# One signal a tile for the left-over sums of a graph convolution

## The reference

```python
def gcn_conv(x, edge_index, W, b, n_nodes):
    ...
    norm = dinv[src] * dinv[dst]
    h = x @ W.T
    msg = h[src] * norm[:, None]
    out = jax.ops.segment_sum(msg, dst, num_segments=n_nodes)
    return out + b
...
    h = gcn_conv(x, edge_index, W1, b1, N_NODES)
    h = jax.nn.relu(h)
    out = gcn_conv(h, edge_index, W2, b2, N_NODES)
...
    x = x + _L0_gnn_ref(_layernorm(x, axis=-1), edge_index, ...)
    x = x + _L0_ffn_ref(_layernorm(x, axis=-1)[None], ...)[0]
```

## Time and profile before

| | |
|---|---|
| median of three executions | 2862.25 us (2860.14 to 2864.53) |
| the profiled execution, its own time | 2881.27 us |
| its span, first to last instruction | 2879.6 us |
| layer 1, layer 2, rest (from the order of time) | some 1228, 1249, 400 us |
| TensorE matmul busy | 2127.8 us (74%) |
| VectorE busy | 1723.6 us (60%) |
| GpSimd busy | 1683.2 us (58%) |
| ScalarE busy | 531.5 us (18%) |
| moved by DMA | 834.62 MB, mean 290 GB/s |
| chain that ended last | TensorE 36%, issue 23%, VectorE 12%, DMA 9%, GpSimd 9% |

### The profile page before, as it was taken

One profiled execution on the slowest core, in us unless ns is written; L12 is line 12 of the kernel. 1 busy time (PEld: TensorE's weight loads), 2 busy tenths in 40 slices (PEclk: granted clock), 3 DMA queues, 4 the chain that ended last, 5 costly groups with the idle time before them and its releaser, 6 DMA issues.

```text
span 2879.6 us, 27437 instructions
## 1 busy us (share of the span) xinstructions
PE 2127.8 (74%) x7723; PEld 1309.1 (45%) x7724; DVE 1723.6 (60%) x2263; ACT 531.5 (18%) x985; POOL 1683.2 (58%) x1752
## 2 busy tenths in 40 slices
PE   6615777777777777777766777778777777887768
PEld 6603444444444444444434444445444444454534
DVE  8654666655666665566645666565566656655536
ACT  7840101101111010111101111111111111111220
POOL 3246666666666666666656666666666666666300
PEclk9997898888888888988878888898888888888969
DMA  9497888888888888888868988888888888888766
GB/s 339 158 380 270 278 283 290 285 282 294 281 290 282 291 287 286 299 279 284 291 242 280 329 299 302 298 311 299 302 301 299 299 308 314 298 296 324 286 216 262
DMA packets 228816, 834.62 MB, mean 290 GB/s; under 512 B 61676, under 2 KB 62460, under 8 KB 228748
## 3 DMA queue, kind: packets, MB, share of 16 engines
q0 software_dynamic: 135968, 633.20, 63.1%
q1 hardware_dynamic: 64964, 158.63, 15.3%
q10 hardware_dynamic: 27836, 42.21, 4.0%
HBM read 784.81 MB, written 81.21 MB: 301 GB/s over the span
## 4 chain that ended last, share of the span: by engine, by line
PE 36%; issue 23%; DVE 12%; DMA 9%; POOL 9%; another core or an unknown queue 6%; ACT 3%; DVEq 1%; POOLq 0%; SPq 0%; ACTq 0%
PE work L1411 15%; PE left L1440 13%; DVE acc L1159 8%; DMA rows<-table_layer,gidx 7%; POOL rows L684 5%; POOL rows L691 3%; PE fixed L1398 2%; PE work L1426 2%; ACT logits L756 1%; ACT xsT L745 1%; PE fixed L1387 1%; DVE hot L1117 1%; PE acc L1547 1%; PE fixed L1547 1%
## 5 line engine op out<-in xcount | busy, mean ns | idle before, releaser
L1159 DVE TENSOR_TENSOR acc<-acc,rows 128x768 f32<-128x768 f32 x1078 | 1038.6, 963 | 761.5 <-DMA rows<-table_layer,gidx 534.7
L684 POOL DMA_INDIRECT rows<-table_layer,gidx x1176 | 1114.3, 948 | 359.9 <-issue 357.2
L1411 PE MATMUL work<-WT,aggT 128*128 128x384 f32 x2352 | 883.6, 538 | 250.4 <-issue 142.0
L1440 PE MATMUL left<-rows,hot 128*128 128x384 f32 x1960 | 826.7, 553 | 237.5 <-issue 235.3
L1411 PEld LDWEIGHTS work<-WT,aggT 128*128 128x128 f32 x2352 | 496.1, 213 | 642.7 <-issue 278.7
L691 POOL DMA_INDIRECT rows<-table_layer,gidx x490 | 490.4, 1001 | 484.9 <-remote 216.7
L1440 PEld LDWEIGHTS left<-rows,hot 128*128 128x128 f32 x1960 | 396.6, 214 | 512.4 <-issue 369.1
L847 ACT ACTIVATE aggT<-fixed 128x768 f32<-128x768 f32 x98 | 79.4, 810 | 1040.1 <-remote 1020.8
L815 ACT ACTIVATE acc<-rows 128x768 f32<-128x768 f32 x98 | 79.8, 815 | 822.2 <-DMA rows<-table_layer,gidx 641.6
L1398 PE MATMUL fixed<-ident,xs 128*128 128x128 f32 x294 | 68.8, 401 | 91.0 <-issue 78.0
L1398 PEld LDWEIGHTS fixed<-ident,xs 128*128 128x128 f32 x294 | 55.7, 213 | 128.1 <-issue 112.8
(11 more groups left out here) (323 smaller groups left out, 1321.1 us busy)
## 6 DMA issues: line engine op xcount, KB each, us to landing
self_row<-table_layer SPq DMA_DIRECT2D x98, 384.0 KB
rows<-table_layer,gidx POOLq DMA_INDIRECT x1666
xstage<-in_x SPq DMA_DIRECT2D x67, 384.0 KB
xs<-in_x SPq DMA_DIRECT2D x58, 384.0 KB
table_layer<-ynext SPq DMA_DIRECT2D x48, 384.0 KB
xnew<-xs SPq DMA_DIRECT2D x47, 384.0 KB
table_layer<-xstage ACTq DMA_DIRECT2D x40, 384.0 KB
rows<-xnew SPq DMA_DIRECT2D x18, 384.0 KB
```

The lines of the kernel that those rows point to most:

```text
L684: pool.indirect_dma_start(rows[:, slot, :], None, table[l][0:ROWS, :], bass.IndirectOffsetOnAxis(ap=gidx[:, k % 2, slot:slot + 1], axis=0) ...
L1159: dve.tensor_tensor(acc[:, :, 0:H], acc[:, :, 0:H], halves(row), ALU.add).then_inc(S["added"], 1)
L1411: m = pe.matmul(work[:, h, 0:H], aggT[:, kc, :], WT[l][:, kc, h * H:(h + 1) * H], start=kc == 0, stop=kc == KC - 1)
L1440: m = pe.matmul(left[:, h, 0:H], hot[:, b, c, :], rows[:, slot, h * H:(h + 1) * H], start=c == 0, stop=c == LEFT - 1)
```

## The change

TensorE increments `left_summed` once a tile, on the last matmul of the fifth left-over sum, in place of once behind each of the five. GpSimd waits for the semaphore once a tile, ahead of the first left-over gather, and for the count of whole tiles; the four waits and register additions between the five gathers go. The two waits of VectorE count tiles too. No DMA and no matmul changes its place, and none is added or left out.

```diff
-                    pool.reg_mov(summed_needed, LEFT * (PEELED - 1) + 1)
+                    pool.reg_mov(summed_needed, PEELED)
...
+                    if not known:
+                        pool.wait_ge(S["left_summed"], summed_needed)
+                        pool.reg_add(summed_needed, summed_needed, 1)
+                    elif t >= 1:
+                        pool.wait_ge(S["left_summed"], t)
                     for r in range(LEFT):
-                        if not known:
-                            pool.wait_ge(S["left_summed"], summed_needed)
-                            pool.reg_add(summed_needed, summed_needed, 1)
-                        elif t >= 1:
-                            pool.wait_ge(S["left_summed"], LEFT * (t - 1) + r + 1)
                         gather_left(r)
...
                     if not (isinstance(t, int) and t < 2):
-                        dve.wait_ge(S["left_summed"], LEFT * (t - 1))
+                        dve.wait_ge(S["left_summed"], t - 1)
...
                         dve.wait_ge(S["added"], OWN * (t + 1))
-                        dve.wait_ge(S["left_summed"], LEFT * (t + 1))
+                        dve.wait_ge(S["left_summed"], t + 1)
...
                             for h in range(2):
                                 m = pe.matmul(left[:, h, 0:H], hot[:, b, c, :], rows[:, slot, h * H:(h + 1) * H],
                                               start=c == 0, stop=c == LEFT - 1)
-                            m.then_inc(S["left_summed"], 1)
+                            if c == LEFT - 1:
+                                m.then_inc(S["left_summed"], 1)
```

## The result

The changed kernel takes 2999.95 us, the median of four runs (2994.4 to 3001.74), against 2861.19 us (2858.02 to 2864.53, four runs) of the kernel before: 1.0482 times as long, 95% interval 1.0463 to 1.05. The forecast was 2979 us, and the case behind it, late and early tiles that take turns, is what happened. The profiled execution took 3001.74 us for a span of 2999.7 us.

A forecast was written before the change was run, and what follows sets the result against it. GpSimd's queue was taken to set the pace of both layers. Lateness of 11 us in layer 1 and 106 us in layer 2, 117 us, put on the median of 2862.25 us gave 2979 us, range 2868 to 3092.

The forecast's parts named there:

- late and early tiles that take turns: Layer 2: tiles whose first left-over gather starts 4.8 us late (29.9 us) alternate with tiles of 25.1 us; chance 0.50.
- The place of the cost: GpSimd, before each tile's first left-over gather, now awaiting the fifth sum: idle time from 484.9 to near 600 us.
- 22 x 4.8 = 106 us: Layer 2: half of some 44 steady tiles start their first left-over gather 4.8 us later, 106 us in all.
- the hold: TensorE's signals to other engines arrive late, 8.5 us in layer 2, until the DMA engines fall idle.
- the two places that the forecast drew on: Start of layer 2, end of layer 1: transposes 10.5 and 11.8 us after a gather, signals through in 0.6 and 1.0.
- 46 x 0.25 = 11 us: Layer 1: the fifth sum ends slightly behind the release, 0.25 us a tile over 46 tiles; bounds 0 and 37 us.
- release: End of the hold, when waiting engines are let go together, some 4.0 us after the last own gather starts.
- The signals, nothing: TensorE: dropping four of five increments a tile, 98 x 4 instructions, is worth nothing on the path.
- The "faster" rival: Signals delivered in a row at the release cost time each; fewer save 24 us, 2838 us; chance 0.06.
- TensorE's stall goes: Layer 1: with four signals under way instead of six, the left-over sums run through without single records; worth nothing.
- The sum on the median: The 117 us were added to the runs' median, 2862.25 us, the profiled execution being 19 us above it.
- TensorE ahead for good: Layer 2 costs nothing because the fifth sum is always ready before the release, or no hold exists; 2873 us, chance 0.12.

The follow-up runs named there:

- e9: The change with only the turn of x moved behind the fifth left-over sum, on a chip with the hold: 2903.14 us, ratio 1.0142.
- e8: The change with both turns (the finished sum's and x's) behind the fifth left-over sum, so the five sums run in one piece: 2894.21 us, ratio 1.003.
- e1: The change with TensorE signalling after each of the five sums again, GpSimd still waiting once, for the fifth: 2672.76 us, ratio 1.0495.
- b_same_again: The kernel before, unchanged, run again for its trace on a chip without the hold: 2554.6 us, a single run.
- e7: The kernel before with only the turn of x moved behind the fifth left-over sum: 2888.18 us, ratio 1.0008.

## Why the prediction was right, and where not

**The place of the cost: right.** GpSimd's queue sets the pace, and the cost sits before a tile's first left-over gather: 607.0 us idle there, forecast near 600.

**Layer 2, 22 x 4.8 = 106 us: right in mechanism and size, on a chip with the hold.** Measured 104.9 us; late tiles 29.9 us (forecast 29.9), early tiles 24.9 to 25.0 (forecast 25.1); waits of 8.6 and 3.7 us (forecast 8.6 and 3.8). e9 shows the cause: with the turn of x out of the way the late tiles vanish. The size holds between the two profiled executions; on the medians it could be up to 18.7 us more.

**Why they take turns: right in outcome, rough in its reason.** Behind a late tile the transposes ended 11.3 us after the first gather (forecast 10.3), and I had said that the signal gets through, as in the earlier trace rows, within some 1 us. It took 5.0 us, still in time for the fifth sum. Behind an early tile they ended 12.7 us after it (forecast 11 to 13.5) and were held 11.4 us. The tiles of layer 2 from the sixth to the forty-fifth are alike: in 20 the transposes ended 10.2 to 11.3 us after the first gather and ScalarE had them 2.5 to 5.7 us later, in 20 they ended 11.9 to 13.7 us after it and were held 10.4 to 12.2 us. But one of the two places that the forecast drew on was misread. Before the change, start of layer 2, POOL:

```profile
1514.86 1.00 POOL L691 DMA_INDIRECT rows<-table_layer,gidx  x1 [0.30 <-issue]
```

This is the first left-over gather of its tile; the one at 1521.39 is the second. From the first, the transposes ended 17.1 us on, further than the 15.9 us at which they are held, and still came through. So the earlier trace rows did not show that the distance decides, and that the tiles take turns as forecast is in this step partly luck. What decides between a short and a long delay I don't know.

**Layer 1, 46 x 0.25 = 11 us: right in mechanism, too small.** The traces have 20.3 us, of which the steady tiles explain 0.31 us a tile (25.45 against 25.14), 14 us in all; the rest lies in the tiles near the layer's ends. The 0.25 came from two tiles of the earlier trace rows, one on time and one 0.8 us late, and was to stand for what slack gives back. The two tiles shown above start 0.9 and 0.5 us later behind their release than before (1.61 and 1.21 in place of 0.69). e8, whose sums run in one piece, has 25.14 us a tile there, as the kernel before.

**The signals, nothing: right without the hold, not separated with it.** e1 gives them back and stays within 0.14 percentage points of the change, though in another group. Both ran on chips without the hold; with it, no run has five signals and the late wait. The "faster" rival, worth 0.06, falls with the result, and with it the rule of the Trainium skill (TensorE: Matmul & The Clock Gate, The cost: per-tile semaphore tail), one increment at the end, as a gain here: 4 x 98 x 0.026 = 10 us was the estimate by its figure, and no run shows a gain.

**TensorE's stall goes: right in the main.** Idle time before the left-over sums fell from 237.5 to 33.9 us; that no single record is left was too strong (834.99). The stall needs the hold and not only the signals: with five signals a tile and no hold it is 24.2 us (b_same_again) and 23.6 (e1).

**The sum on the median: the weakest step.** 117 us of terms meet 120.1 us between the profiled executions. On the medians it is 138.8. I put the sum on the median as if the 19 us above it were the same in both kernels; in the changed kernel they are 2. The medians would allow layer 1 to cost up to some 40 us.

**"TensorE ahead for good" as the case without a hold: wrong.** I wrote that with no hold there is no chain, and 2873 us. Without the hold the kernel before is 11% faster, GpSimd issues back to back, and then the four sums of 1.33 us themselves are in the way: 5% slower again. I priced a missing hold at the pace of the held kernel. The slack that covered the fifth sum, 3.8 us of waiting in every tile, was the hold's own.

## What to carry to other kernels

Merging signals into one saves nothing unless the signals cost something, and it moves the wait to the last of them: before doing it, list all that stands on the producer's queue between the first signal and the last, other waits above all. If one signal is wanted, move what waits out of the way first (e8: 0.3% slower, where the change itself was 4.5 to 4.8% slower on other chips with the hold). An idle gap on the bounding engine is cover only as long as its cause stays, so price the edit with the gap and without.

## What the runs showed of the hardware that I had not expected

The same kernel took 2548, 2861 and 2885 us on different chips. In the traces the difference goes with the delivery of TensorE's signals under indirect gathers: 0.03 us after the transposes in the trace of the kernel before at 2554.6 us, at a DMA share of 0.98; in the one at 2881.27 us the middle value is 5.5 us in layer 1 and 9.2 us in layer 2, and in that of e7, on the chip of 2885 us, 5.5 and 9.9 us. By the Trainium skill (SBUF — State Buffer, Who interferes with whom) DMA never contends with a compute engine: the 0.03 us agree with it, the 5.5 to 9.9 us are a delay that it does not speak of, since its rule is about the ports of SBUF; the prediction was too quick to call it the opposite. Waiting for the same thing costs the same 5% for two different reasons. Why chips differ in this, what ends a hold when the DMA engines are still 90% busy, and whether the late signals and the stops of TensorE in e8 have one cause, stays open; nothing that I ran separates them.
